# An RWKV-6 layer with a routed expert layer on one core: ScalarE's copy of an expert's tokens goes in front of two other copies, VectorE empties an expert's PSUM bank in front of two masked copies, W2 is loaded behind the first bias, and GpSimd normalises one token tile in four

## The reference, cut to what matters

```
xn  = layernorm(x)
out = x + attention(xn) + experts(xn)

attention:  x_last = xn shifted by one token; b_a = x_last - xn
            h   = tanh((xn + b_a*miu_x) @ A)            # 5 groups of 32 codes per token
            miu = h_s @ Bp_s + lam_s ;  in_s = xn + b_a*miu_s   (s = w,k,v,r,g)
            w = td_miu + tanh(w_in @ tdA) @ tdB
            k = (k_in @ Wk.T) * exp(min(w,0)); v = v_in @ Wv.T; r = r_in @ Wr.T
            g = tanh(g_in @ Wg1) @ Wg2
            per head of 64:  y_t = r_t (S + u k_t v_t);  S <- S*exp(w_t) + k_t v_t
            groupnorm(y)*gamma + beta, times g, @ Wo.T
experts:    top-1 of 8:  (relu(xn @ W1[e] + b1[e]) @ W2[e] + b2[e]) * prob
```

## Time and profile before

| | |
|---|---|
| median of 3 runs | 611.93 us (611.58 to 612.84) |
| the profiled execution: its time, its span | 612.62 us, 611.3 us |
| TensorE matmul, weight load | 545.2 us (89%), 483.0 us (79%) |
| VectorE | 449.7 us (74%) |
| ScalarE | 339.4 us (56%) |
| GpSimd | 187.7 us (31%) |
| mean granted TensorE clock | 0.982 of full speed |
| chain that ended last | TensorE 61%, VectorE 17%, issue 8%, ScalarE 7%, DMA 3% |

### The profile page before, as it was taken

One profiled execution on the slowest core, in us unless ns is written; L12 is line 12 of the kernel. 1 busy time (PEld: TensorE's weight loads), 2 busy tenths in 40 slices (PEclk: granted clock), 3 DMA queues, 4 the chain that ended last, 5 costly groups with the idle time before them and its releaser, 6 DMA issues.

```text
span 611.3 us, 18795 instructions
## 1 busy us (share of the span) xinstructions
PE 545.2 (89%) x7278; PEld 483.0 (79%) x7278; DVE 449.7 (74%) x1124; ACT 339.4 (56%) x753; POOL 187.7 (31%) x148
## 2 busy tenths in 40 slices
PE   2779797979999999999999899999999999989974
PEld 2557686868888888889798788888897988878873
DVE  6979999978577685948576876859485767768552
ACT  4874663245655656564645456575646465554751
POOL 4401010121243252344342332523433423423233
PEclk9998898989999999999999999999999999999998
DMA  8969543895333314142342223241432433221233
GB/s 282 280 239 300 157 126 97 257 358 130 71 53 85 46 39 97 34 96 46 70 70 72 44 71 45 53 81 35 95 45 74 66 72 46 53 35 33 26 51 43
DMA packets 49802, 60.75 MB, mean 99 GB/s; under 512 B 5057, under 2 KB 44098, under 8 KB 49570
## 3 DMA queue, kind: packets, MB, share of 16 engines
q1 hardware_dynamic: 36898, 44.72, 25.6%
q0 software_dynamic: 11840, 14.42, 15.7%
q10 hardware_dynamic: 976, 0.41, 0.2%
HBM read 40.79 MB, written 23.07 MB: 104 GB/s over the span
## 4 chain that ended last, share of the span: by engine, by line
PE 61%; DVE 17%; issue 8%; ACT 7%; DMA 3%; POOL 1%; ACTq 1%; DVEq 0%; SPq 0%; POOLq 0%
PE F L656 11%; PE F L664 8%; PE G L465 7%; PE LL L524 7%; PE G L497 4%; PE G L481 4%; PE YB L589 3%; DVE mix L1016 3%; PE G L434 2%; PE YB L587 2%; ACT AT L1473 2%; DMA out<-rows,dst_row 2%; PE YB L625 1%; DVE small L815 1%; PE YB L615 1%
## 5 line engine op out<-in xcount | busy, mean ns | idle before, releaser
L1730 POOL DMA_INDIRECT out<-rows,dst_row x39 | 65.5, 1681 | 237.8 <-DVE rows L1145 226.4
L656 PEld LDWEIGHTS F<-xsT,w1s 128*128 128x128 f32 x624 | 73.8, 192 | 22.1 <-ACT xsT L1515 12.2
L656 PE MATMUL F<-xsT,w1s 128*128 128x128 f32 x624 | 78.0, 278 | 14.3 <-ACT xsT L1515 9.8
L1016 DVE SCALAR_TENSOR_TENSOR mix<-G,vec,ba 128x256 f32<-128x256 f32 x160 | 69.6, 476 | 19.1 <-PE G L434 19.1
L664 PE MATMUL F<-w,hsT 128*128 x312 | 75.1, 383 | 1.0 <-issue 0.6
L1077 DVE TENSOR_TENSOR RK<-RK,D 128x256 f32<-128x256 f32 x112 | 47.2, 421 | 35.4 <-issue 27.1
L1533 ACT ACTIVATE hsT<-F,b1c 128x128 f32<-128x128 f32 x156 | 44.5, 368 | 50.8 <-PE F L656 50.8
L664 PEld LDWEIGHTS F<-w,hsT 128*128 128x128 f32 x312 | 57.1, 190 | 9.4 <-issue 1.5
L1055 DVE COPY_PREDICATED AP_<-msk,LL 128x256 f32<-128x256 uint32 x96 | 51.1, 532 | 15.1 <-issue 11.1
L1024 DVE TENSOR_TENSOR mix<-mix,xnT 128x512 f32<-128x512 f32 x80 | 55.1, 689 | 1.5
L1716 POOL DMA_INDIRECT rows<-xn_d,src_row x39 | 40.5, 1039 | 36.5 <-PE F L645 19.6
(11 more groups left out here) (180 smaller groups left out, 1203.3 us busy)
## 6 DMA issues: line engine op xcount, KB each, us to landing
cd<-cd_d SPq DMA_DIRECT2D x30, 320.0 KB, 5.5
w<-in_W SPq DMA_DIRECT2D x16, 512.0 KB, 8.1
cd_d<-w SPq DMA_DIRECT2D x32, 160.0 KB, 2.9
b2t<-in_b SPq DMA_DIRECT2D x39, 128.0 KB
w<-in_x SPq DMA_DIRECT2D x8, 512.0 KB, 9.7
xn_d<-w SPq DMA_DIRECT2D x8, 512.0 KB
out<-in_x SPq DMA_DIRECT2D x8, 512.0 KB, 5.3
out<-res POOLq DMA_DIRECT2D x16, 256.0 KB, 4.7
```

The costliest lines, as they stand in the source:

```text
L656: i1 = pe.matmul(FB[:, k * P:(k + 1) * P], w1s[:, cc, k, :], xsT[:, cc, :], start=(cc == 0), stop=(cc == 1))
L1016: i1 = dve.scalar_tensor_tensor(mixed_in(u, c, n, cc), bk[:, cc * UN:(cc + 1) * UN], cvec(LAM + CC * n, cc), ba[:, cc, :, :].rearrange("p ...
L1730: pool.indirect_dma_start(io["out"], bass.IndirectOffsetOnAxis(dst_row[:, f:f + 1], 0), ys[:, f % 2, :], None, compute_op=ALU.add).then_in ...
```

## The change: what it does

Four edits in the engines' orders.

1. **ScalarE and TensorE, in a round.** `spread` and `bonus` leave the end of a round. In the next round `spread` stands behind `tokens(fa)`, and `bonus` behind `rectified(fa)` and `decay_down`. Where fa is None, TensorE does `read_out` directly behind `key_back`, in front of `decay_down`, `state` and `mixed 2`.
2. **ScalarE and VectorE, later in a round.** `saved(32)` goes in front of `last_bias(fc)`. On VectorE `grow(16)` and `expert_out(fb)` go in front of levels 2 and 3, and `gated` behind `grow(32)` and `added 4`.
3. **SyncE.** The wait for `ex` and `bias(0)` go in front of the wait for `inv` and the eight loads of W2.
4. **Start.** Of VectorE's two tiles a round, GpSimd takes the second, behind its `pow` (new semaphore `xnp`, which all readers of `xtok` and the reuse of the statistics wait for).

```diff
 def half(h):                      # TensorE
     key_back(u, c)
     if fa is not None:
         hidden(fa)
+    else:
+        read_out(u, c, 0)
+        read_out(u, c, 1)
     decay_down(u, c + 1)
     state(u, c)
     mixed(u, c + 1, 2)
-    read_out(u, c, 0)
-    read_out(u, c, 1)
+    if fa is not None:
+        read_out(u, c, 0)
+        read_out(u, c, 1)
...
 def normalise(j):                 # VectorE
-    for t in (2, 3):
-        i1 = dve.tensor_scalar(xtok[:, 4 * j + t, :], xall[:, 4 * j + t, :], mv[:, t, 0:1], rs[:, t:t + 1], ALU.subtract, ALU.mult)
-    i1.then_inc(s["xnd"])
+    dve.tensor_scalar(xtok[:, 4 * j + 2, :], xall[:, 4 * j + 2, :], mv[:, 2, 0:1], rs[:, 2:3], ALU.subtract, ALU.mult).then_inc(s["xnd"])
...
 def half(h):                      # VectorE
     mixed(u, c + 1, 4)
-    levels(*v, 2, 3)
     grow(*v, 16)
     if fb is not None:
         expert_out(fb)
-    levels(*v, 4)
-    gated(u, c)
+    levels(*v, 2, 3, 4)
     grow(*v, 32)
     added(u, c + 1, 4)
+    gated(u, c)
     grow(*v, 64)
...
 def half(h):                      # ScalarE
     if fa is not None:
         tokens(fa)
+    spread(u, c)
+    if fa is not None:
         last_bias(fa)
     key_back(u, c)
     if fa is not None:
         rectified(fa)
     decay_down(u, c + 1)
-    if h == 1:
-        bonus(0, 1)
+    bonus(*v)
...
         tokens(fc)
+    saved(*v, 32)
+    if fc is not None:
         last_bias(fc)
-    saved(*v, 32)
...
     out(u, c)
-    if h < NU - 3:
-        spread(*v)
-        bonus(u, c + 1)
...
+def normalise(j):                 # GpSimd
+    st, mv, rs, nm = moments_of(j)
+    pool.wait_ge(s["rs"], j + 1)
+    pool.tensor_scalar(xtok[:, 4 * j + 3, :], xall[:, 4 * j + 3, :], mv[:, 3, 0:1], rs[:, 3:4], ALU.subtract, ALU.mult).then_inc(s["xnp"])
...
 for j in range(NJ):
     inverse_deviation(j)
+    normalise(j)
...
+sp.wait_ge(s["ex"], 1)            # SyncE
+bias(0)
 sp.wait_ge(s["inv"], 1)
 for e in range(E):
     sp.dma_start(w2[:, e * HC * C:(e + 1) * HC * C].rearrange("p (c n) -> p c n", c=HC),
                  io["W2"][e].rearrange("(c p) n -> p c n", p=P)).then_inc(s["ew2"], 16)
-sp.wait_ge(s["ex"], 1)
-bias(0)
```

More of the change, by code:

```diff
@@ L182, in program @@
         s = {n: ctx.enter_context(nc.semaphore("s_" + n)) for n in (
-            "cv cn c1 c2 w x0 x1 x2 x3 x4 x5 x6 x7 xk ck0 ck1 ck2 z_pool omx bn ag ve rs nm xna xnd tr tc sc lg xx hm h hi lo "
+            "cv cn c1 c2 w x0 x1 x2 x3 x4 x5 x6 x7 xk ck0 ck1 ck2 z_pool omx bn ag ve rs nm xna xnd xnp tr tc sc lg xx hm h hi lo "
             "four hg hf hc cx ls lgc lgt bst cst wvc ew1 ew2 "
@@ L338, in ln_transpose @@
                 pe.wait_ge(s["xnd"], j + 1)
+                pe.wait_ge(s["xnp"], j + 1)
                 if j == 0:
@@ L819, in moments @@
                     dve.wait_ge(s["xna"], j - 1)
+                    dve.wait_ge(s["xnp"], j - 1)
                 for t in range(4):
@@ L1345, in scaled @@
                     act.wait_ge(s["xnd"], NJ)
+                    act.wait_ge(s["xnp"], NJ)
                 for cc in range(CC):
@@ L1352, in scaled_half @@
                 act.wait_ge(s["xnd"], NJ - 1)
+                act.wait_ge(s["xnp"], NJ - 1)
                 for cc in range(CC):
@@ L1657, in scalar_program @@
             block(1, 0)
-            spread(1, 0)
             for h in range(1, NU - 2):
@@ L1852, in sync_program @@
                 sp.wait_ge(s["xnd"], j + 1)
+                sp.wait_ge(s["xnp"], j + 1)
                 sp.dma_start(xkr[j, :, :, :], xtok[:, 4 * j:4 * j + 4, :]).then_inc(s["xk"], 16)
```

## The result

The changed kernel took 591.27 us (median of 4; 590.4 to 594.01) beside 612.38 us (4; 611.58 to 614.2) for the kernel before on the same chip: ratio 0.9659, 95% interval 0.962 to 0.9698. I had forecast 597.5 and a range of 594 to 604. The direction was right; the time lies under the range. The profiled execution took 590.40 us (span 589.1), 22.2 less than the one of before.
The time of the kernel before depends on the chip: about 612 to 615 us on this one and on chips 3 and 10, 603.5 on chips 0 and 8. Medians are over all runs of a kernel and ratios over its fast ones (one run of `b_gather_late` and one of the kernel before on chip 3 were slow).

A forecast was written before the change was run, and what follows sets the result against it. TensorE bounds a round: busy 32.51 of 34.00 us. Terms -9.8 + 0.6 - 2.5 - 1.7 - 1.5 = -14.9 us from 612.62 gave 597.7, forecast 597.5, range 594 to 604.

The forecast's parts named there:

- Edit 1, ten rounds (forecast -9.8): Rounds with fa: copying tokens first ends TensorE's 0.97 us wait for ScalarE's xsT at hidden, 9.8 us in ten rounds.
- the rival of `key_back`: Wait moves to state, which needs key_back behind more ScalarE copies; ten rounds give back 0.6 us each, 603.5 us; 16%.
- Edit 1, rounds 1, 7, 13 (forecast +0.6): Rounds without fa: read_out fills the decay_down gap but no longer covers decay_up; net +0.2 us a round, +0.6 in three.
- Edit 2 (forecast -2.5): TensorE's wait at hidden(fc) for VectorE to empty bank FB goes, 2.5 us in ten rounds.
- The third is touched by nothing: TensorE's twelve waits inside L524 (last_levels), 3.5 us, marked as unaffected by any edit.
- my sum was 14.9: All terms of the four edits together: 14.9 us faster.
- Edit 4 (forecast -1.7): Start: giving GpSimd one tile shortens VectorE's rounds by 0.33 us, 2.0 in six, less 0.3: 1.7 us won.
- The tile's 1.23 us was mis-sized: Start: GpSimd's tile was taken as 0.55 us, fitting behind a pow of 1.17 in a round of 2.3.
- I took 0.3 off: Start, last tile: 0.3 us deducted because GpSimd and VectorE keep each other from SBUF.
- Edit 3 (forecast -1.5): Later W2 loads stop disturbing TensorE's last_levels and clock near 128 to 139 us; 1.5 us taken, cause not shown.
- a bound (4.0): Most that W2's later loading could win: 1.2 us of holes and 2.8 of lower clock.

The follow-up runs named there:

- b_gather_late: Kernel before, with GpSimd's gather tokens(fc + 2) behind difference instead of in front of it; 629.7 us, ratio 1.0449, on chip 8.
- e1_all: Kernel before with edit 1 alone; 594.6 us, ratio 0.9886, on chip 8.
- e2: Kernel before with edit 2 alone; 600.47 us, ratio 0.9961, on chip 8.
- a_gather_in3: Changed kernel with GpSimd's gather tokens(fc + 2) held until grow(32), so that it runs within last_levels; 598.49 us, ratio 0.9744, on chip 10.
- b_gather_first: Kernel before, with GpSimd's gather of tile fc+2 in front of the scatter of tile fb; 637.55 us, ratio 1.0346, on chip 10.
- e4: Kernel before with edit 4 alone; 611.96 us beside 615.26, ratio 0.995, on chip 3.
- e3: Kernel before with edit 3 alone; 613.8 us, ratio 0.9997, on chip 3.
- before_p: The kernel before itself, run unchanged for its profile on chip 0; 603.59 us.
- a_old_read_out: Changed kernel with read_out back behind mixed 2 in rounds 1, 7 and 13; 585.87 us, ratio 0.9722 (chip 0), 587.75 us, 0.9582 (chip 10).

## Why the prediction was too cautious

**Edit 1, ten rounds (forecast -9.8).** Right in mechanism. None of the copies behind the waiting one was late; the rival of `key_back` didn't come. The size was off: 1.13 us a round, not 0.97. The wait ran from the end of L569's matmuls, but a matmul that isn't waiting starts before the one in front of it ends: L657 now starts at 296.00, 0.16 before L570's 296.16. So -11.3. `e1_all` gives the same 1.13.

**Edit 1, rounds 1, 7, 13 (forecast +0.6).** In 7 and 13 the wait moved from `decay_down` to `decay_up` (1.06 us, I had said 0.9) and to `value`, as worked out: undoing the order gave 0.15 back in each, and I had said +0.2. With edit 2's part and the gap these rounds gain 0.75 and 0.9. In round 1 the step failed: I priced it at the clock of the other rounds. `read_out` now stands in the low clock, where its 2.7 us take 5.3 (133.08 to 138.39), and waits 1.08 us for `spread` first. Round 1 lost 2.3 us; undoing the order gave 3.3 back in one pair of traces, about 3 by all traces of the changed kernel, and 1.8 to 2.4 in the medians.

**Edit 2 (forecast -2.5).** The wait went, again with the overlap on top: `hidden(fc)` starts 0.39 us sooner instead of 0.25, so -3.9. In `e2` a round is 0.46 shorter, so -4.6; where the other 0.07 lies isn't shown.

**"The third is touched by nothing": the step that failed most.** What went with it was 0.42 to 0.55 us in each of twelve rounds, 5.6 us. I had read an "issue" wait as TensorE's own. But edit 2 moves `expert_out(fb)` forward, by that the scatter of fb, and by that the gather behind it on GpSimd. I had followed VectorE's and ScalarE's queues from the moved step, not GpSimd's. `a_gather_in3` shows the tie to the gather's place, and `b_gather_first` agrees; that it was edit 2 that moved the gather is read from the timelines, as edit 2 alone didn't run on a chip with the gap. What in the gather stops TensorE, and why only on some chips, stays open. On a chip without the gap the change gives 15.9 us, and my sum was 14.9. That the two are so near is partly luck: the ten rounds gave 15.9 where I had 12.3, and round 1 took back what I had not priced.

**Edit 4 (forecast -1.7).** Measured: round 1 starts 2.6 us sooner after than before, 2.7 sooner in `e4` than in `e3`, and alone the ratio is 0.995. Six start rounds, 0.29 each, are 1.7 of it; VectorE's last tile took 0.41 us, where the pair had taken 1.97. The tile's 1.23 us was mis-sized by a factor of two and cost nothing, since `pow` and tile just fit in the round. VectorE's tile went only from 0.41 to 0.46: that GpSimd holds VectorE here, for which I took 0.3 off, was wrong. The rule of the Trainium skill (GPSIMD Engine Reference, section 8, Key points) that I cited agrees with these traces: VectorE's statistics and their aggregation, with one input each, take 1.39 and 0.38 us beside GpSimd's `pow` and tile as they did beside the `pow` alone (1.40 and 0.38), while the two-input products and GpSimd's subtraction hold each other (0.42 to 2.44 us). At the end of the loop GpSimd's last tile took 1.60 us instead of 1.23 beside VectorE's `cast`, which took 0.98 instead of 0.81 and has one input; whether that `cast` ran in a 2-port mode, as the rule would want, no trace shows.

**Edit 3 (forecast -1.5).** The mechanism was wrong: holes and low clock are there without W2's transfer, and in `before_p` the transfer is there without them. No gain can be told in the times. I had taken a share of a bound (4.0) whose cause no row showed.

By terms: in the ten rounds with fa -11.3 for edit 1, -4.6 for edit 2 and -4.5 for the gap; in rounds 7 and 13 -1.65, which hold the other 1.1 of the gap; +2.3 for round 1, -2.6 for the start and +0.2 for the rest: -11.3 - 4.6 - 4.5 - 1.65 + 2.3 - 2.6 + 0.2 = -22.15 of the 22.2 measured.

## What to carry to other kernels

When a step moves, follow every queue that its result releases, GpSimd's DMA issues too: a wait marked "issue" on TensorE may belong to what another engine starts at that moment. A wait that goes gives back its length and the overlap that matmuls without a wait have (0.14 to 0.16 us each here, against ends that are modelled). Before matmuls are moved into a stretch, look at its granted clock, and before a GpSimd computation moves, by itself or behind a moved gather, look at which VectorE instruction it will run beside.

## What the hardware showed

- On the chips where the kernel before takes 612 to 615 us, a GpSimd gather issued within a dense run of 64x64 matmuls goes with a gap in them, which makes `last_levels` 2.06 us instead of 1.52; with the gather issued 0.39 us ahead of the run it is 1.61. On the two chips where the kernel takes 603.5 there is no gap. In the profiled executions of before on either kind of chip (spans 611.3 and 602.4) the gaps come to 9.7 us: 2.2 in round 0, 0.8 in round 1, 6.7 in rounds 2 to 13.
- GpSimd's two-input subtraction of 128x512 beside VectorE's two-input product of 128x256: 1.06 becomes 1.61 us and 0.42 becomes 2.44 us, more than the two durations one after the other (1.48).
- TensorE's granted clock was 0.50 (1.2 GHz) for 3.4 us (`b_gather_late`) to 13.7 us (`e4`) behind the idle stretch at the end of round 0, with and without DMA traffic. It stayed at 1.00 there in the profiled executions of the kernel before and of `a_old_read_out` on chip 0, with as much idleness (1.83 and 1.78 busy of 3 us); in the latter it fell later, to 0.50 at 150.0 us for 3.4 us, behind the stop of 2.61. So idleness comes before the fall each time, but does not bring it each time.
